# Attention and expert kernel on one core: loading the last stage's first contexts and inputs piece by piece in the last head pair, and dividing them on Pool behind key step 51

## The reference, cut to what matters

```
x = x + layernorm(attention(layernorm(x)))       # causal, softmax over keys
x = x + layernorm(experts(layernorm(x)))         # 2 of 8 experts per batch, chosen
                                                 # by the batch's first token
scores = q @ k^T * SCALE; weights = softmax(where(causal, scores, -inf))
context = weights @ v;  attention = context @ wo + bo
experts: scores0 = x[:, 0, :] @ Wr + br; sum of W2[e] @ gelu(W1[e] @ x) over the 2 best / 2
```

## Time and profile before

| what | value |
|---|---|
| median of 3 runs | 1973.89 us |
| the profiled execution, its own time | 1975.9 us |
| its span, first to last instruction | 1974.2 us |
| PE busy | 98% of the span |
| DVE busy | 90% |
| ACT busy | 69% |
| POOL busy | 15% |
| mean granted clock of PE | 0.995 of full |

### The profile page before, as it was taken

How to read it: one execution, slowest core, us unless ns; L and a number is a source line. 1 busy time by engine, 2 the same in 40 slices (tenths; PEclk the granted TensorE clock), 3 DMA queues, 4 the chain that set the end, 5 groups by cost and what they waited for, 6 DMA issues and landing times. The chain is left out here.

```text
span 1974.2 us, 39435 instructions
## 1 busy us (share of the span) xinstructions
PE 1939.4 (98%) x15684; PEld 850.2 (43%) x15684; DVE 1783.2 (90%) x3574; ACT 1363.5 (69%) x1655; POOL 294.5 (15%) x358
## 2 busy tenths in 40 slices
PE   9999999999999999999999999999999998999998
PEld 6655333333333333333333333333333342667665
DVE  7877899999999999999999999999998985799984
ACT  5766777777777777777777777777777768333432
POOL 4332201111111101011111101010111111322000
PEclk9999999999999999999999999999999999999999
DMA  6876615040414324050503233040506213344321
GB/s 178 252 231 202 146 47 97 7 94 11 90 34 75 58 43 94 9 93 7 94 25 82 41 62 78 22 94 9 93 18 148 61 50 114 87 127 124 94 68 43
DMA packets 151706, 162.93 MB, mean 83 GB/s; under 512 B 58466, under 2 KB 124386, under 8 KB 151522
## 3 DMA queue, kind: packets, MB, share of 16 engines
q1 hardware_dynamic: 146658, 151.98, 32.5%
q0 software_dynamic: 4864, 8.44, 2.0%
HBM read 100.03 MB, written 60.29 MB: 81 GB/s over the span
## 5 line engine op out<-in xcount | busy, mean ns | idle before, releaser
L627 DVE TENSOR_REDUCE b_pmax<-b_ring 128x1 f32<-128x512 f32 (+3 forms) x2264 | 1318.2, 647 | 51.6 <-PE b_ring L617 38.7
L1341 ACT ACTIVATE b_prob<-b_psS 128x1024 f32<-128x1024 f32 (+3 forms) x1280 | 1084.5, 895 | 341.2 <-PE b_psS L1384 337.4
L1384 PE MATMUL b_psS<-g_qT,g_kT 64*128 64x512 bf16 (+7 forms) x5120 | 811.3, 347 | 11.3 <-ACT b_prob L1341 5.5
L617 PE MATMUL b_ring<-g_kT,g_qT 64*128 64x512 bf16 (+3 forms) x2478 | 706.6, 347 | 0.1
L1401 PE MATMUL b_psO<-b_prob,g_v 128*32 128x512 f32 (+3 forms) x5120 | 597.0, 541 | 0.3 <-POOL b_prob L1311 0.3
L1384 PEld LDWEIGHTS b_psS<-g_qT,g_kT 64*128 64x128 bf16 (+1 forms) x5120 | 291.9, 94 | 321.1 <-ACT b_prob L1341 177.9
L617 PEld LDWEIGHTS b_ring<-g_kT,g_qT 64*128 64x128 bf16 x2478 | 221.8, 94 | 384.0 <-DVE b_pmax L627 317.4
L1311 POOL TENSOR_SCALAR_AFFINE_SELECT b_prob<-b_prob 128x512 f32<-128x512 f32 x256 | 162.4, 634 | 1275.0 <-ACT b_prob L1341 1274.9
L615 PE MATMUL b_ring<-later,query_of 64*128 64x128 bf16 x982 | 186.5, 219 | 0.8 <-ACT a_v L1097 0.5
L1401 PEld LDWEIGHTS b_psO<-b_prob,g_v 128*32 128x32 f32 x5120 | 102.9, 108 | 168.5 <-issue 133.2
L1755 PE MATMUL c_psH<-c_yT,c_w1e 128*128 128x512 f32 x256 | 118.3, 611 | 10.0 <-ACT c_hT L1676 7.0
(11 more groups left out here) (162 smaller groups left out, 1060.3 us busy)
## 6 DMA issues: line engine op xcount, KB each, us to landing
qk_parts<-a_parts SPq DMA_DIRECT2D x64, 384.0 KB, 4.5
g_qT<-qk_parts SPq DMA_DIRECT2D x184, 128.0 KB, 4.3
g_kT<-qk_parts SPq DMA_DIRECT2D x184, 128.0 KB, 5.5
out_sums<-b_outT SPq DMA_DIRECT2D x64, 256.0 KB, 2.8
v_ones<-a_v SPq DMA_DIRECT2D x16, 544.0 KB, 6.0
g_v<-v_ones SPq DMA_DIRECT2D x32, 272.0 KB, 5.4
a_x<-in_L_attn_x SPq DMA_DIRECT2D x16, 512.0 KB, 5.3
c_x<-in_L_attn_x SPq DMA_DIRECT2D x15, 512.0 KB, 4.9
```

Of the source, the lines that this page charges most:

```text
L617: ins_ = self.nc.tensor.matmul(to, groups.qT[own, g, h // 2, 0, t * P:(t + 1) * P], groups.kT[own, g, h // 2, 0, pc * CH:pc * CH + w], sta ...
L627: self.nc.vector.tensor_reduce(pmax[:, c % 2].rearrange("p (h t) n -> p h t n", t=TT)[:, heads[0]:heads[-1] + 1:2, qt, pc], bank[:, 0:k * ...
L1341: nc.scalar.activation(prob[:, j % PBUF, 2 * s:2 * s + 2, off:CH], psS[:, 2 * s:2 * s + 2, off:CH], ACT.Exp).then_inc(exp_done, 1)
L1384: ins_ = nc.tensor.matmul(psS[:, 2 * s + p, off:CH], kT[own, g, s, ab, kt * P:(kt + 1) * P], qT[own, g, s, ab, c * CH + off:(c + 1) * CH], ...
```

## The change

The loads of batch 0's contexts are cut into their halves. A new function `load_half_ctx` issues two DMAs (one half of a chunk's contexts and its inverses). Eight of them stand at key steps 18, 21, 24 and so on to 39 of the last pair; the three inputs stand one each at steps 42, 45 and 48. Nothing is added or taken from the bytes that are moved. POOL divides all four chunks behind the mask of step 51. The later loads of inputs (`load_next_inputs`) wait also until both DMAs on one input semaphore have landed.

```
         for k in range(KD):
-            heads = bass.ds(b * H + k * 2 * HG, 2 * HG)
-            eng.dma_start(self.cc[:, c, k], ...).then_inc(done, 16)
-            eng.dma_start(self.inv[:, c, k], ...).then_inc(done, 16)
+            self.load_half_ctx(eng, b, c, k, done)
...
-FRONT_LOAD_AT = 16
-FRONT_DIVIDE_AT = {23: (0, 1), 51: (2, 3)}
+FRONT_LOAD_AT = 18
+FRONT_LOAD_EACH = 3
+FRONT_DIVIDE_AT = 51
...
     def load_next_inputs(self, sp):
         sp.wait_ge(self.x1_done, 2)
+        sp.wait_ge(self.chunks.x_ld[0], 2 * 16)
...
-                if FRONT_LOAD_AT <= at < FRONT_LOAD_AT + NC and last:
-                    if at == FRONT_LOAD_AT:
+                n, rest = divmod(at - FRONT_LOAD_AT, FRONT_LOAD_EACH)
+                if last and rest == 0 and 0 <= n < NC * KD:
+                    if n == 0:
                         sp.wait_ge(chunks.inv_stored, 16 * 2)
-                    front.load_contexts(sp, at - FRONT_LOAD_AT)
-                if at == FRONT_LOAD_AT + NC and last:
-                    front.load_inputs(sp)
+                    front.load_contexts(sp, n)
+                if last and rest == 0 and NC * KD <= n < NC * KD + ROOTED:
+                    front.load_input(sp, n - NC * KD)
...
-                if it == NPAIR - 1:
-                    for n in FRONT_DIVIDE_AT.get(j - it * BK, ()):
+                if j == (NPAIR - 1) * BK + FRONT_DIVIDE_AT:
+                    for n in range(FRONT):
                         front.divide_contexts(pool, n)
```

More of the change, by code:

```diff
@@ L247, in load_ctx, with load_half_ctx @@
         for k in range(KD):
-            heads = bass.ds(b * H + k * 2 * HG, 2 * HG)
-            eng.dma_start(self.cc[:, c, k], self.o_scr[heads, 0:HD, c * CH:(c + 1) * CH]).then_inc(done, 16)
-            eng.dma_start(self.inv[:, c, k], self.inv_scr[heads, c * CH:(c + 1) * CH].unsqueeze(1)
-                          .to_broadcast([2 * HG, HD, CH])).then_inc(done, 16)
+            self.load_half_ctx(eng, b, c, k, done)
+    def load_half_ctx(self, eng, b, c, k, done):
+        heads = bass.ds(b * H + k * 2 * HG, 2 * HG)
+        eng.dma_start(self.cc[:, c, k], self.o_scr[heads, 0:HD, c * CH:(c + 1) * CH]).then_inc(done, 16)
+        eng.dma_start(self.inv[:, c, k], self.inv_scr[heads, c * CH:(c + 1) * CH].unsqueeze(1)
+                      .to_broadcast([2 * HG, HD, CH])).then_inc(done, 16)
     LOADS = 4
@@ L717, with load_contexts, load_input @@
     LOGITS_AT = 2 * FRONT + 4
[L720 to L725, removed]
+    def load_contexts(self, sp, n):
+        self.chunks.load_half_ctx(sp, 0, n // KD, n % KD, self.chunks.first_ld)
+    def load_input(self, sp, n):
+        if n < 2:
             self.chunks.load_x(sp, n, n)
-        sp.dma_start(self.attn[:, :, :], self.chunks.x_t[2]).then_inc(self.chunks.x_ld[0], 16)
+        else:
+            sp.dma_start(self.attn[:, :, :], self.chunks.x_t[2]).then_inc(self.chunks.x_ld[0], 16)
     def load_next_contexts(self, sp, c):
```

## The result

| | before | changed |
|---|---|---|
| median of 9 runs | 1973.89 us (1971.79 to 1978.52) | 1968.59 us (1965.89 to 1970.81) |
| ratio, 95% interval | | 0.9964 (0.9954 to 0.9974) |
| profiled execution, span | 1974.2 us | 1964.2 us |
| stretch between the masks of steps 20 and 36, last pair | 44.54 us | 37.46 us |
| PE's wait for `g_qT<-shifts` | 4.25 us | none |

The kernel is faster by 0.36% (0.26 to 0.46), 5.3 us by the medians and 7.1 us by the ratio. Predicted were 1967.2 us, in a range from 1965.8 to 1971.0.

The account below looks back on a forecast made before the run. With PE and DVE nearly full, the removable loss was PE's 4.25 us wait for shifts behind context DMAs, plus its slow clock afterwards. Gain 6.7 us, other terms 0: median 1973.9 to 1967.2 us, range 1965.8 to 1971.0.

Parts of the forecast that it names:

- The one wait: Last pair, key step 24: PE's scores matmul waits 4.2 us for `g_qT<-shifts`, held behind context DMAs; the wait goes.
- SP's clumps: SP's queue, last pair: SP has nothing to wait for at step 18, so every third step is no spacing in time.
- The shifts' new landing: Shifts of (g 0, c 3): line 654 issued near 1519.2, rows there near 1521.6, 3.4 us of slack before PE.
- The size: Last pair, masks of steps 20 to 36: gain 6.7 us (44.54 - 37.83), bounds 6.2 to 7.6.
- twin: The same stretch in an earlier pair, taken as the length without the stall: pair 6, 37.83 us; pairs 1 to 6, 36.90 to 38.30.
- The other pieces, the inputs, POOL, the new wait: 0: Later pieces, inputs, four divisions behind step 51 and the wait in `load_next_inputs`: each counted as costing 0.
- From the sum to the median: Whole kernel: the 6.7 us gain reaches the end, so the median goes from 1973.9 to 1967.2 us.
- pays less: Rival: the stall goes but is shorter without a profile; gain 2 to 5.5 us, 1971.9 to 1968.4; chance 0.22.
- The queue's start and rate: SP's queue ahead of the shifts: DMAs move 171 GB/s, queue empty near 1510, seven us before the shifts' issue at 1517.04.
- The wait moves: Rival: a piece still holds the shifts of (g 0, c 3) or others; 0 to 3 us gained, about 1972.5; chance 0.06.
- the divisions come late: Rival: POOL's divisions wait for a late last piece and PE stands 11.5 us; 1981.2 us; chance 0.03.

Follow-up runs that it names:

- ten ahead: Changed kernel with its pieces from step 14 on, one at every step, so 10 context DMAs precede the shifts; median 1973.9 us, ratio 1.0002.
- held: Changed kernel with one SP wait added, issuing the shifts of (g 0, c 3) only after key step 23's scores; median 1974.7 us, ratio 0.9999.
- sixteen: Kernel before with FRONT_LOAD_AT = 15, all 16 context DMAs ahead of the shifts; median 1980.6 us, ratio 1.0020.
- the second series: Changed kernel timed again, against 26 runs of the kernel before (median 1976.3 us); median 1968.7 us, ratio 0.9961.
- 8 DMAs ahead: Kernel before with FRONT_LOAD_AT = 17, 8 context DMAs ahead of the shifts instead of 12; median 1968.2 us, ratio 0.9976.
- the one-constant one: Kernel before with FRONT_LOAD_AT = 19 for 16, the whole context burst behind the shifts of (g 0, c 3); median 1968.8 us, ratio 0.9961.

## Why the prediction was right, point by point

*The one wait.* Right. It was found in the list of waits, and it is gone; moving the burst behind the shifts does the same, and holding the shifts back brings the wait and the whole cost back.

*SP's clumps.* Right: the first piece was issued at 1502.27, the pieces of 27 and 30 directly behind each other, as were those of 33 to 39. Every third step is no spacing in time.

*The shifts' new landing.* I had SP's line 654 (659 in the changed kernel) near 1519.2 and it came at 1518.38 (with everything 0.5 us earlier): right.

*The size.* I took 6.7 us from pair 6 as twin, the stretch became 7.08 us shorter, between 6.7 and the upper 7.6. The sum of the parts, 4.25 + 6.08 / 2 = 7.3, was nearer. The clock's part is in fact about half of the time worked at 0.50: 2.8 for 6.1 us, 5.7 for 12.2 us with ten ahead, 2.5 for 5.1 us when held, 2.0 for 4.3 us with sixteen. The twin was a little too long for a measure: the stretch came down to 37.46 us and not to its 37.83. That fits DVE's work, 36.59 us in the twin, 36.12 in the stretch of before and 35.79 in the changed one; the first two were in the rows and I left the difference out.

*The other pieces, the inputs, POOL, the new wait: 0.* Right, each stretch from step 36 to 76 kept its length to 0.02 us. One reading was off and did no harm: of the three stores behind the inputs only two are issued together, the third comes 17.5 us later in the changed kernel. The burst behind the shifts is the harder test, with 23 us of lateness at a later shift, which cost nothing.

*From the sum to the median.* Predicted 1967.2, measured 1968.6. That is in the range, but above the 1966.3 to 1967.7 of the forecast itself and above the 1968.0 to which I gave 0.64: it lies in the part of the range that was there for the rival "pays less". So the mechanism was right, and that the median stayed inside owes something to the width. With 7.1 us in the stretch, the medians differ by 5.3; the ratios give 7.1 and, in the second series, 7.7. One argument was wrong: against a stall that varies I set that two of three runs agreed within 0.2 us. In 26 runs the kernel before goes from 1970.9 to 1982.7 (in 25 on another chip from 1968.4 to 1979.7), while the changed one stays within 1965.9 to 1970.8 in its sixteen. The median of before, on which the forecast stands, was itself 1973.9, 1976.3 and 1974.8 in the three series. The stall measured 4.25, 5.18 and 5.71 us in three profiles with the same queue. So a good part of the scatter of before fits this queue; that all of it does was not shown, as stage C varies by 2 us on its own.

*The queue's start and rate.* Here a term was wrong, though it did not decide. I had reckoned with one rate, 171 GB/s, and a burst that starts as in the one profile, and so expected 8 DMAs ahead to be free. The piece of 0.5 MB was safe, but by less than the 7 us I claimed. In the first profile the DMAs had fallen to 10 GB/s by 1510 to 1512, about 6 us ahead of the shifts. In the second its first issue took 5.2 us, its second DMA was issued only at 1508.3, and 101 GB/s still moved from 1512 to 1514, with the shifts at 1517.2, at least 3 us later.

*The rivals.* "Pays less" was not what happened in the trace, though the medians alone would allow it. "The wait moves" and "the divisions come late" did not occur.

Of the versions that are faster than the kernel before, the changed one and the one-constant one are equal: 1968.65 and 1968.77 us on one chip. Eight ahead has a median of 1968.2 on another chip, at a ratio of 0.9976 with an interval that holds theirs; its trace still has the wait. No run was clearly faster than the changed kernel.

## What to carry to other kernels

A tiny transfer that the critical engine waits for shares its queue with everything issued before it: look in the list of waits for a DMA of a few KB with a wait of several us, and see what stands ahead of it. Here it was enough to move the bulk loads behind it, with one constant. Whether spreading them pays where there is no such place, no run here shows. Cost a stall of PE as its idle time plus half of the time that PE then works at the lower clock, read both from rows of the stall itself, and take more than one profile: equal queues gave 4.25 to 5.71 us here.

## What the runs showed of the hardware that I had not expected

- PE's granted clock stayed at 1.00 behind 1.65 us of idling. Behind 3.08 us it fell to 0.50 for about 3 us of work, behind 4.25 to 5.71 us for 4 to 12 us. The length does not follow the idle time: behind 4.35 us of idling PE worked 12.2 us at the lower level (1.2 GHz), behind 16.47 us 4.3 us. In the latter run the clock was at 0.50 for the last 11.7 us of the idle time too, where it costs nothing.
- Most issues of a 256 KB context DMA took SP 0.57 us. From the tenth of sixteen in a row on they took 1.6 to 2.1 us, and the first one behind the group's loads 2.8 to 5.7 us (0.64 where it came 18 us behind them). Whatever SP had to issue next was delayed by that; that a full queue is the cause is my reading, no row names it.
